# One fused Mamba and mixture-of-experts block: C rows spread by DMA, the front by chunks, one product per pair in the second batch

## The chip, the cores and the metric

One core of one Trainium2 chip. A time is the device time of one execution in microseconds (us); lower is better. TensorE, VectorE, ScalarE, GpSimd (POOL) and the DMA-issuing SyncE (SP) have an instruction queue each, run in their own order, and meet only at semaphores.

## What is computed

The input is (2, 128, 16, 16): two batches of 256 tokens with 128 channels. Cut to what matters:

```python
x = x + L0_conv(ln_c(x))                       # Mamba layer: the part that the change edits
t = t + L0_ffn(ln_t(t))                        # 8 experts, top 2, width 512, gelu
x = x + L1_conv(ln_c(x), A)                    # decay along tokens
t = t + L1_ffn(ln_t(t))                        # 16 experts, top 2, width 256

# L0_conv, per batch, T=256 tokens, D_INNER=256 (two chunks of 128), 16 states:
xin, z = split(layernorm(x) @ in_proj_w.T)
xc = silu(causal_conv4(xin) + conv_b)
dt_raw, Bm, Cm = split(xc @ x_proj_w.T, [8, 16, 16])
dt = softplus(dt_raw @ dt_proj_w.T + dt_proj_b);  A = -exp(A_log)
h_t = exp(dt_t * A) * h_(t-1) + (dt_t * xc_t) * B_t        # for each of 16 states
y_t = sum_n h_t[n] * C_t[n] + xc_t * D
out = layernorm(clamp((y * silu(z)) @ out_proj_w.T))
```

## The kernel before

**Stages.** The *front* (about 0 to 30 us) normalises both batches, builds fused convolution weights `w_tap` (in_proj times taps) and does batch 0's convolution, step sizes `dt` and rows B and C. The *scan stage* (about 30 to 110 us) walks the 16 states of batch 0 and then of batch 1 in 8 pairs each; pair m = k + 8b counts through both. Batch 1's own convolution, gate and `dt` run inside batch 0's pairs, and batch 0's output, norms and router inside batch 1's. The *expert stage* (about 110 us to the end) runs four passes of 16 units, where TensorE does three products per hidden chunk (`hidden`, L1068 to L1070) and the second layer (`output`, L1092).

**Order.** A list `plan` names steps with arguments; every engine walks the same list and runs the steps it has a function for, so the list fixes each queue's order. `b1_in`, `b1_c` and `b1_out` insert batch 1's steps into batch 0's pairs.

**A pair.** TensorE spreads two B rows over the partitions by transposing a broadcast column of `bc_tok` (`spread_b`, L968) into one PSUM bank `bc_ps[0]`, and two C rows into `bc_ps[1]` (`spread_c`). ScalarE makes the decays `da` (four Exp, L487, a ring of four buffers) and copies the C rows to `cb` (L495, a ring of two). VectorE multiplies `dtx` by the B rows (`inputs`, L674) and runs the scan (`states`, L684); in pair m it does `inputs(m+1)` ahead of `states(m)`. POOL multiplies scan and `cb` (`weigh`, L326); TensorE sums the result into y (`add`, L986), one pair later.

**Front.** TensorE spreads the taps and the dt bias by products with a single row of ones (L889, L925), and does `keep_warm` products (L875) that nobody reads. ScalarE's activation functions lie in tables, and a change of set is an ACT_TABLE_LOAD; the kernel brings one in early with a dummy activation (L419, L437). `softplus(b)` is Abs, Exp (L447), Ln (L449) on ScalarE, with the rounding error of 1 + e corrected on VectorE (L648 to L653 for batch 0; `rounding`, L664 and L665, for batch 1, whose rest, `step_1` and `step_x`, is POOL's).

## Time and profile before

| | us |
|---|---|
| median of three runs | 230.44 |
| lowest, highest | 229.32, 231.79 |
| profiled execution, its own time | 230.71 |
| its span, first to last instruction | 228.9 |

The page of the profile sums each engine's busy time, cuts the span into 40 slices, follows the chain of work that ended last, and lists groups of instructions. The trace behind it answers for a stretch: which instruction ran when on which engine, and what ended the idle time before it. Busy time is an average over stages with different limits, so each stage is read by itself. The two "x" numbers of an instruction merged with its neighbours are one start and one total.

### The profile page before, as it was taken

The page shows a single profiled execution, that of the slowest core. Times are in us where ns is not written, and L with a number is a line of the kernel's source. Part 1 is how long each engine was busy: PE and PEld are TensorE (multiplying, and loading weights), DVE is VectorE, ACT ScalarE, POOL GpSimd, SP SyncE. Part 2 cuts the span into 40 slices and gives each one's busy share as a digit, 9 for nine tenths or more (in the row PEclk, how much of TensorE's full clock was granted, in tenths as well). Part 3 has the DMA queues.
Part 4 walks back from the last instruction along what each step waited for, and adds up shares of the span by engine and source line. Part 5 has one row for each costly group of instructions (what it writes and reads, how often), then busy time and mean ns, then how long its engine had stood idle before and what let it go on. Part 6 is the DMA issues. An engine that isn't in the chain of part 4 may idle for free. (4 is left out here: it accounts for less than half of the span.)

```text
span 228.9 us, 3874 instructions
## 1 busy us (share of the span) xinstructions
PE 197.1 (86%) x1272; PEld 164.4 (72%) x1272; DVE 133.9 (59%) x312; ACT 130.1 (57%) x290; POOL 104.5 (46%) x136
## 2 busy tenths in 40 slices
PE   7987598889467785967999999969999999999993
PEld 4565477546143542435699998969998899999993
DVE  2624275998256999999327474546325774433342
ACT  2502995993994481566247774746755556455630
POOL 5301004475373978463926643542436444354410
PEclk9999959999959998899999999979999999999999
DMA  5999960000000000000000000000000000000000
GB/s 144 303 334 319 315 189 0 1 1 0 0 3 0 0 1 0 0 0 0 3 0 0 6 0 0 3 0 3 0 0 1 3 3 3 0 26 0 0 3 23
DMA packets 6164, 9.65 MB, mean 42 GB/s; under 512 B 369, under 2 KB 2937, under 8 KB 6146
## 3 DMA queue, kind: packets, MB, share of 16 engines
q1 hardware_dynamic: 6146, 9.42, 13.7%
q8 instruction: 10, 0.16, 0.3%
q14 instruction: 8, 0.07, 0.1%
HBM read 9.16 MB, written 0.26 MB: 41 GB/s over the span
## 5 line engine op out<-in xcount | busy, mean ns | idle before, releaser
L326 POOL TENSOR_TENSOR hc<-hs,cb 128x1024 f32<-128x1024 f32 x16 | 37.6, 2352 | 40.4 <-DVE hs L684 40.4
L809 DVE SCALAR_TENSOR_TENSOR acc<-dbx_ps,comb,acc 128x128 f32<-128x128 f32 x96 | 29.1, 345 | 38.0 <-PE dbx_ps L1092 36.9
L1068 PE MATMUL bc_ps<-x_hi,w_hi 128*128 128x256 f32 x128 | 42.1, 329 | 0.0
L540 ACT ACTIVATE hid<-bc_ps,par 128x256 f32<-128x256 f32 x64 | 26.9, 471 | 22.0 <-PE bc_ps L1070 21.9
L684 DVE TENSOR_TENSOR_SCAN hs<-da,dbx_ps 128x1024 f32<-128x1024 f32 x16 | 36.5, 2279 | 1.4 <-ACT da L487 0.8
L1070 PE MATMUL bc_ps<-x_hi,w_lo 128*128 128x256 f32 x128 | 36.5, 285 | 0.0
L968 PEld LDWEIGHTS bc_ps<-ident,bc_tok 128*128 128x128 f32 x128 | 16.4, 152 | 27.9 <-ACT cb L495 9.4
L1069 PE MATMUL bc_ps<-x_lo,w_hi 128*128 128x256 f32 x128 | 36.4, 284 | 0.0
L340 POOL TENSOR_TENSOR w_lo<-w1b,w_hi 128x256 fp32r<-128x256 f32 x32 | 23.5, 735 | 27.6 <-ACT w_hi L532 27.3
L968 PE MATMUL bc_ps<-ident,bc_tok 128*128 128x128 f32 x128 | 21.3, 301 | 16.8 <-DVE dbx_ps L674 7.4
L1092 PE MATMUL dbx_ps<-w2a,hid 128*128 128x128 f32 x256 | 35.0, 281 | 0.5 <-issue 0.3
L1092 PE MATMUL dbx_ps<-w2b,hid 128*128 128x128 f32 (+1 forms) x256 | 33.9, 276 | 0.5 <-DVE acc L809 0.5
L340 POOL TENSOR_TENSOR w_lo<-w1a,w_hi 128x256 fp32r<-128x256 f32 x32 | 23.2, 731 | 23.0 <-ACT w_hi L532 23.0
L1092 PEld LDWEIGHTS dbx_ps<-w2a,hid 128*128 128x128 f32 x256 | 32.2, 196 | 1.2 <-ACT hid L540 0.6
L543 ACT ACTIVATE hid<-bc_ps 128x512 f32<-128x512 f32 x32 | 19.1, 597 | 24.0 <-PE bc_ps L1070 23.9
L1092 PEld LDWEIGHTS dbx_ps<-w2b,hid 128*128 128x128 f32 x256 | 31.3, 191 | 1.0 <-issue 0.7
L487 ACT ACTIVATE da<-dt,a_neg 128x255 f32<-128x255 f32 x64 | 27.1, 497 | 0.0
L1068 PEld LDWEIGHTS bc_ps<-x_hi,w_hi 128*128 128x128 f32 x128 | 24.7, 193 | 0.6 <-issue 0.5
L1069 PEld LDWEIGHTS bc_ps<-x_lo,w_hi 128*128 128x128 f32 x128 | 24.7, 193 | 0.5 <-issue 0.5
L1070 PEld LDWEIGHTS bc_ps<-x_hi,w_lo 128*128 128x128 f32 x128 | 24.6, 192 | 0.0
L674 DVE TENSOR_TENSOR dbx_ps<-dtx,bc_ps 128x1024 f32<-128x1024 f32 x16 | 19.6, 1224 | 7.1 <-POOL dtx L362 3.7
L986 PE MATMUL y_ps<-hc,ident 128*128 128x512 f32 x32 | 17.0, 658 | 2.9 <-POOL hc L326 2.9
(164 smaller groups left out, 247.2 us busy)
## 6 DMA issues: line engine op xcount, KB each, us to landing
w1a<-w_in SPq DMA_DIRECT2D x2, 1024.0 KB, 9.5
w1b<-w_in SPq DMA_DIRECT2D x2, 1024.0 KB, 11.8
par<-packed_in SPq DMA_DIRECT2D x1, 472.0 KB, 3.5
x_cm<-x_in SPq DMA_DIRECT2D x2, 128.0 KB, 2.3
y_out<-out_sb SPq DMA_DIRECT2D x2, 128.0 KB, 1.7
w2a<-w_in SPq DMA_DIRECT2D x2, 0.5 KB, 9.8
w2b<-w_in SPq DMA_DIRECT2D x2, 0.5 KB, 10.1
row_sb<-row_in SPq DMA_DIRECT2D x1, 5.0 KB
```

Source lines behind the costliest of these rows:

```text
L326: nc.gpsimd.tensor_tensor(hc[p][:], hs[p][:], cb[p][:].rearrange("p i (o t) -> p i o t", o=1).to_broadcast([128, PAIR, DC, T]), ALU.mult). ...
L340: nc.gpsimd.tensor_tensor(w1_lo[p][:], w1[layer][:, bass.ds(u * UW, UW)], w1_hi[p][:].bitcast(F32), ALU.subtract).then_inc(s["w1_staged"], 1)
L487: ins = nc.scalar.activation(da[q][:, i, c, 1:T], dt[:, c, b, 1:T], ACT.Exp, scale=a_neg[:, c * NS + k * PAIR + i:c * NS + k * PAIR + i + 1])
L540: ins = nc.scalar.activation(hid[p][:, c, :], h_ps[:, p, T * c:T * (c + 1)], ACT.Gelu, bias=par[:, bass.ds(u * UC + at, 1)])
L674: nc.vector.tensor_tensor(dbx[p], dtx[b][:].rearrange("p (o c) t -> p o c t", o=1).to_broadcast([128, PAIR, DC, T]), rows.to_broadcast([12 ...
L684: nc.vector.tensor_tensor_scan(*flat, 0.0, ALU.mult, ALU.add).then_inc(s["h_done"], 1)
L809: nc.vector.scalar_tensor_tensor(acc[k][:, t, :], o_ps[:, w // span % RING, 128 * t:128 * (t + 1)], comb[layer][b][:, t, bass.ds(u, 1)], a ...
L968: ins = nc.tensor.transpose(bc_ps[which][:, T * i + 128 * t:T * i + 128 * (t + 1)], bc_tok[:, b, t, n:n + 1].to_broadcast([128, 128]), ide ...
L1068: nc.tensor.matmul(h_ps[:, p, T * c:T * (c + 1)], w1_hi[w][:, at], x_hi[b][:], start=True, stop=False)
L1069: nc.tensor.matmul(h_ps[:, p, T * c:T * (c + 1)], w1_hi[w][:, at], x_lo[b][:], start=False, stop=False)
L1070: ins = nc.tensor.matmul(h_ps[:, p, T * c:T * (c + 1)], w1_lo[w][:, at], x_hi[b][:], start=False, stop=True)
L1092: ins = nc.tensor.matmul(o_ps[:, bank, 128 * t:128 * (t + 1)], hid[p][:, c, 128 * t:128 * (t + 1)], w2[layer][:, bass.ds(u * UC + c, 1), : ...
```

## The change

- **C rows.** ScalarE copies the 16 C rows of a batch to `c_row` (16 partitions); SP stores them to a small DRAM tensor and loads them back, spread over 128 partitions, in three parts (pairs 0, 1 to 3, 4 to 7) into a `cb` that holds all 8 pairs. `spread_c`, the `cb` copies and their semaphores go. SP does this after the first half of layer 0's weights, and for batch 1 after all weights.
- **Front.** The taps come by a DMA that spreads one row over 128 partitions (into `cb`'s last slots) and a ScalarE copy into PSUM; the dt bias is added by ScalarE and VectorE as a column of the packed parameters. `xs_a` lives in PSUM. Four `keep_warm` products instead of nine after `rows_out`. `conv(0)` and `conv(1)` follow one another; `softplus(0)` goes by chunks of 128 channels, each in its own bank.
- **Tables** are loaded by name, without dummy activations.
- **Batch 1.** The copies `u1` and `z0` go; silu reads PSUM. `v(1)` moves from after pair 4 to after pair 2, `bc(1)` from after pair 2 to after pair 3, `bc_copy(1)` from pair 4 to pair 5 behind `softplus(1)`, `rounding` and `step_1` from after pair 5 to after pair 4, `step_x` from after pair 6 to after pair 5. `rounding` waits for Exp and not for Ln.

The diff, cut to its core:

```diff
+C_PARTS = ((0, 1), (1, 4), (4, NP))
...
-plan = [("constants",), ("x_stats", 0), ("x_stats", 1), ("rows_out",), ("x_norm", 0), ("taps", 0), ("inner_x", 0),
-        ("taps", 1), ("in_proj", 0), ("conv", 0), ("x_norm", 1), ("inner_x", 1), ("conv", 1), ("in_proj", 1),
-        ("v", 0), ("bc", 0), ("z", 0), ("softplus", 0), ("bc_copy", 0), ("z_copy",), ("first_rows",),
-        ("conv1", 0), ("second_b",), ("conv1", 1), ("second_c",)]
-b1_in = {3: [("silu1",)], 4: [("bc_copy", 1)]}
-b1_c = {1: [("conv1_copy",)], 5: [("softplus", 1)]}
-b1_out = {1: [("z", 1)], 2: [("bc", 1)], 4: [("v", 1)], 5: [("rounding",), ("step_1",)], 6: [("step_x",)]}
+plan = [("constants",), ("x_stats", 0), ("x_stats", 1), ("rows_out",), ("taps_in", 0), ("x_norm", 0), ("taps_in", 1),
+        ("taps", 0), ("inner_x", 0), ("taps", 1), ("in_proj", 0), ("x_norm", 1), ("conv", 0), ("conv", 1), ("inner_x", 1),
+        ("in_proj", 1), ("v", 0), ("bc", 0), ("softplus", 0), ("first_rows",), ("z", 0), ("conv1", 0), ("second_b",),
+        ("conv1", 1), ("first_sum",)]
+b1_in = {3: [("silu1",)], 5: [("softplus", 1), ("bc_copy", 1)]}
+b1_out = {1: [("z", 1)], 2: [("v", 1)], 3: [("bc", 1)], 4: [("rounding",), ("step_1",)], 5: [("step_x",)]}
 for k in range(NP):
-    plan += [("pair_in", 0, k)] + b1_in.get(k, []) + [("pair_c", 0, k)] + b1_c.get(k, [])
-    plan += [("pair_out", 0, k)] + b1_out.get(k, [])
+    plan += [("pair_in", 0, k)] + b1_in.get(k, []) + [("pair_out", 0, k)] + b1_out.get(k, [])
 for k in range(NP):
-    plan += [("pair_in", 1, k)] + [(name, 0, 0) for name in before_states.get(k, [])] + [("pair_c", 1, k)]
+    plan += [("pair_in", 1, k)] + [(name, 0, 0) for name in before_states.get(k, [])]
...
+    sp.dma_start(cb[:, NP - DC:NP].rearrange("p c i t -> p (c i t)"), taps.to_broadcast([C, DC * TAPS * 128])).then_inc(s["taps_loaded"], 16)
...
+    def c_rows_round(b):
+        sp.wait_ge(s["c_row_ready"], b + 1)
+        sp.dma_start(c_rows[b], c_row[:, b, :]).then_inc(s["c_row_stored"], 16)
+        sp.wait_ge(s["c_row_stored"], 16 * (b + 1))
+        for i, (k0, k1) in enumerate(C_PARTS):
+            if b:
+                sp.wait_ge(s["hc_done"], k1 + RING)
+            sp.dma_start(cb[:, k0:k1].rearrange("p k i t -> p (k i t)"),
+                         c_rows[b, PAIR * k0:PAIR * k1].rearrange("(o n) t -> o (n t)", o=1).to_broadcast([128, (k1 - k0) * PAIR * T])
+                         ).then_inc(s[f"c{i}_loaded"], 16)
+    weights(0, 0, w1_0, w2_0)
+    c_rows_round(0)
+    weights(0, 1, w1_0, w2_0)
+    for i in range(2):
+        weights(1, i, w1_1, w2_1)
+    c_rows_round(1)
...
     def weigh(b, k, p):
         m = k + NP * b
         pool.wait_ge(s["h_done"], m + (1 + RING))
-        pool.wait_ge(s["cb_done"], m + (1 + RING))
+        for i, (k0, k1) in enumerate(C_PARTS):
+            if k0 <= k < k1:
+                pool.wait_ge(s[f"c{i}_loaded"], 16 * (b + 1))
         pool.wait_ge(s["y_done"], m + 1)
         nc.gpsimd.tensor_tensor(hc[p][:], hs[p][:],
-                                cb[p][:].rearrange("p i (o t) -> p i o t", o=1).to_broadcast([128, PAIR, DC, T]),
+                                cb[:, k].rearrange("p i (o t) -> p i o t", o=1).to_broadcast([128, PAIR, DC, T]),
...
     def constants():
+        nc.scalar.preload_act_table_set("exp_and_others")
         act.wait_ge(s["params_loaded"], 16)
         nc.scalar.activation(a_neg[:], col("a_log"), ACT.Exp).then_inc(s["a_exp"], 1)
+        nc.scalar.preload_act_table_set("silu_and_others")
         act.wait_ge(s["ident_ready"], 1)
         for c in range(DC):
             ins = nc.scalar.activation(diag_d[:, c, :], ident[:], ACT.Identity, scale=col("d_skip")[:, c:c + 1])
         ins.then_inc(s["diag_ready"], 1)
-        act.wait_ge(s["ones_ready"], 1)
-        link(nc.scalar.activation(scrap[:], ones[:, 0:1], ACT.Silu))
...
+    def taps_in(c):
+        act.wait_ge(s["taps_loaded"], 16)
+        nc.scalar.activation(taps_ps[c], taps_sb[:, c, :], ACT.Copy).then_inc(s["taps_ps"], 1)
...
     def softplus(b):
         if b == 0:
-            logarithm_table()
-        act.wait_ge(s["dt_ps"], b + 1)
-        link(nc.scalar.activation(dt_a[b][:], halves(dt_ps[b]), ACT.Abs))
-        if b:
-            nc.scalar.activation(dt[:, :, b, :], halves(dt_ps[b]), ACT.Relu)
-        nc.scalar.activation(dt_e[b][:], dt_a[b][:], ACT.Exp, scale=-1.0).then_inc(s["exp_dt"], 1)
-        act.wait_ge(s["exp_dt"], b + 1)
-        nc.scalar.activation(dt_l[b][:], dt_e[b][:], ACT.Ln, bias=ones[:, 0:1]).then_inc(s["ln_dt"], 1)
+            for c in range(DC):
+                act.wait_ge(s["dt_ps"], c + 1)
+                nc.scalar.activation(dt_a[0][:, c], dt0_ps[c][:, 0:T], ACT.Abs, bias=dt_bias(c)).then_inc(s["abs_done"], 1)
+                act.wait_ge(s["abs_done"], c + 1)
+                nc.scalar.activation(dt_e[0][:, c], dt_a[0][:, c], ACT.Exp, scale=-1.0).then_inc(s["exp_dt"], 1)
+            nc.scalar.preload_act_table_set("natural_log")
+            bc_copy(0)
+            for c in range(DC):
+                act.wait_ge(s["exp_dt"], c + 1)
+                nc.scalar.activation(dt_l[0][:, c], dt_e[0][:, c], ACT.Ln, bias=ones[:, 0:1]).then_inc(s["ln_dt"], 1)
+            nc.scalar.preload_act_table_set("exp_and_others")
+            return
+        act.wait_ge(s["dt_ps"], DC + 1)
+        for c in range(DC):
+            ins = nc.scalar.activation(dt_a[1][:, c], halves(dt1_ps)[:, c, :], ACT.Abs, bias=dt_bias(c))
+        ins.then_inc(s["abs_done"], 1)
+        for c in range(DC):
+            ins = nc.scalar.activation(dt[:, c, 1, :], halves(dt1_ps)[:, c, :], ACT.Relu, bias=dt_bias(c))
+        ins.then_inc(s["relu_done"], 1)
+        act.wait_ge(s["abs_done"], DC + 1)
+        nc.scalar.activation(dt_e[1][:], dt_a[1][:], ACT.Exp, scale=-1.0).then_inc(s["exp_dt"], 1)
+        nc.scalar.preload_act_table_set("natural_log")
+        act.wait_ge(s["exp_dt"], DC + 1)
+        nc.scalar.activation(dt_l[1][:], dt_e[1][:], ACT.Ln, bias=ones[:, 0:1]).then_inc(s["ln_dt"], 1)
+        nc.scalar.preload_act_table_set("exp_and_others")
...
     def bc_copy(b):
         act.wait_ge(s["bct_ps"], b + 1)
-        nc.scalar.activation(bc_tok[:, b], bct_ps[b], ACT.Copy).then_inc(s["bct_ready"], 1)
-    def z_copy():
+        nc.scalar.activation(c_row[:, b, :], bct_ps[b][0:NS, T:2 * T], ACT.Copy).then_inc(s["c_row_ready"], 1)
+        nc.scalar.activation(b_tok[:, b], bct_ps[b][:, 0:TT * NS].rearrange("p (t r) -> p t r", t=TT),
+                             ACT.Copy).then_inc(s["bct_ready"], 1)
+    def silu1():
+        nc.scalar.preload_act_table_set("silu_and_others")
         act.wait_ge(s["z_ps"], 1)
-        nc.scalar.activation(z0[:], halves(z_ps[0]), ACT.Copy).then_inc(s["z_copied"], 1)
-    def conv1_copy():
+        nc.scalar.activation(sz[:, :, 0, :], halves(z_ps), ACT.Silu).then_inc(s["sz_ready"], 1)
         act.wait_ge(s["conv1_ps"], 1)
         for c in range(DC):
-            ins = nc.scalar.activation(u1[:, c, :], halves(conv1_ps)[:, c, :], ACT.Identity, bias=col("conv_b")[:, c:c + 1])
-        ins.then_inc(s["u1_ready"], 1)
-    def silu1():
-        act.wait_ge(s["u1_ready"], 1)
-        nc.scalar.activation(xc[:, :, 1, :], u1[:], ACT.Silu).then_inc(s["xc_ready"], 1)
-        act.wait_ge(s["z_copied"], 1)
-        nc.scalar.activation(sz[:, :, 0, :], z0[:], ACT.Silu).then_inc(s["sz_ready"], 1)
+            ins = nc.scalar.activation(xc[:, c, 1, :], halves(conv1_ps)[:, c, :], ACT.Silu, bias=col("conv_b")[:, c:c + 1])
+        ins.then_inc(s["xc_ready"], 1)
         act.wait_ge(s["z_ps"], 2)
-        nc.scalar.activation(sz[:, :, 1, :], halves(z_ps[1]), ACT.Silu).then_inc(s["sz_ready"], 1)
...
-    def c_rows(b, k, p):
-        m = k + NP * b
-        act.wait_ge(s["c_ready"], m + 1)
-        act.wait_ge(s["hc_done"], m + 1)
-        nc.scalar.activation(cb[p][:], bc_ps[1].rearrange("p (i t) -> p i t", i=PAIR),
-                             ACT.Copy).then_inc(s["cb_done"], 1)
...
     def inner_x(b):
         at = slice(TT * b, TT * (b + 1))
-        normalise(TT, xs_b[:, at, :], xs_a[:, at, :], mv[b], rstd_b[b], "rstd2", b).then_inc(s["xs_tok"], 1)
+        dve.wait_ge(s["xtok_ready"], b + 1)
+        normalise(TT, xs_b[:, at, :], xs_a[b], mv[b], rstd_b[b], "rstd2", b).then_inc(s["xs_tok"], 1)
...
-        dve.wait_ge(s["exp_dt"], 1)
-        nc.vector.scalar_tensor_tensor(dt_q[0][:], halves(dt_ps[0]), 0.0, dt_e[0][:], ALU.max, ALU.add)
-        link(nc.vector.tensor_scalar(dt_a[0][:], dt_e[0][:], 1.0, 1.0, ALU.add, ALU.subtract))
-        link(nc.vector.tensor_tensor(dt_q[0][:], dt_q[0][:], dt_a[0][:], ALU.subtract))
-        dve.wait_ge(s["ln_dt"], 1)
         for c in range(DC):
-            nc.vector.tensor_tensor(dt[:, c, 0, :], dt_q[0][:, c], dt_l[0][:, c], ALU.add).then_inc(s["dt0_ready"], 1)
+            g, low, e = dt_q[0][:, c], dt_a[0][:, c], dt_e[0][:, c]
+            dve.wait_ge(s["abs_done"], c + 1)
+            nc.vector.tensor_scalar(g, dt0_ps[c][:, 0:T], col("dt_b")[:, c:c + 1], 0.0, ALU.add, ALU.max).then_inc(s["r_done"], 1)
+            dve.wait_ge(s["exp_dt"], c + 1)
+            dve.wait_ge(s["r_done"], c + 1)
+            nc.vector.tensor_tensor(g, g, e, ALU.add)
+            link(nc.vector.tensor_scalar(low, e, 1.0, 1.0, ALU.add, ALU.subtract))
+            link(nc.vector.tensor_tensor(g, g, low, ALU.subtract))
+            dve.wait_ge(s["ln_dt"], c + 1)
+            nc.vector.tensor_tensor(dt[:, c, 0, :], g, dt_l[0][:, c], ALU.add).then_inc(s["dt0_ready"], 1)
...
     def rounding():
-        dve.wait_ge(s["ln_dt"], 2)
-        link(nc.vector.tensor_scalar(halves(y_ps), dt_e[1][:], 1.0, 1.0, ALU.add, ALU.subtract))
-        nc.vector.tensor_tensor(dt_q[1][:], halves(y_ps), dt_e[1][:], ALU.subtract).then_inc(s["rounded"], 1)
+        dve.wait_ge(s["exp_dt"], DC + 1)
+        dve.wait_ge(s["relu_done"], 1)
+        link(nc.vector.tensor_scalar(halves(f_ps), dt_e[1][:], 1.0, 1.0, ALU.add, ALU.subtract))
+        nc.vector.tensor_tensor(dt_q[1][:], halves(f_ps), dt_e[1][:], ALU.subtract).then_inc(s["rounded"], 1)
...
-        pe.wait_ge(s["ones_ready"], 1)
-        pe.wait_ge(s["row_loaded"], 16)
-        for c in range(DC):
-            nc.tensor.matmul(taps_ps[c], ones[0:1, 0:128], row_sb[0:1, DI + 512 * c:DI + 512 * (c + 1)],
-                             start=True, stop=True).then_inc(s["taps_ps"], 1)
         pe.wait_ge(s["rows_loaded"], 16)
         for c in range(DC):
             ins = nc.tensor.matmul(wv_ps[:, T * c:T * (c + 1)], rows_sb[:, 128 * c:128 * (c + 1)], rows_sb[:, DI:2 * DI],
                                    start=True, stop=True)
         ins.then_inc(s["wv_ps"], 1)
-        for sem, value in (("var1", 2), ("rstd1", 2), ("var2", 1)):
-            keep_warm(sem, value)
+        for sem, value in (("rstd1", 2), ("var2", 1)):
+            keep_warm(sem, value, 2)
...
+    def v(b):
+        if b == 0:
+            pe.wait_ge(s["wv_ready"], 1)
+            for c in range(DC):
+                pe.wait_ge(s["xc_ready"], c + 1)
+                for j in range(DC):
+                    ins = nc.tensor.matmul(dt0_ps[j][:, 0:T], w_dt[:, c, 128 * j:128 * (j + 1)], xc[:, c, 0, :],
+                                           start=(c == 0), stop=(c == DC - 1))
+                    if c == DC - 1:
+                        ins.then_inc(s["dt_ps"], 1)
+            return
+        pe.wait_ge(s["xc_ready"], DC + 1)
         for j in range(DC):
...
     def bc(b):
...
         pe.wait_ge(s["xc_ready"], DC + b)
         if b:
             pe.wait_ge(s["sz_ready"], NB)
+        else:
+            pe.wait_ge(s["xs_ready"], 1)
         w = col("xproj").rearrange("p (c r) -> p c r", c=DC)
         for t in range(TT):
             for c in range(DC):
-                ins = nc.tensor.matmul(bct_ps[b][:, t, :], xc[:, c, b, 128 * t:128 * (t + 1)], w[:, c, DTR:DTR + BC],
-                                       start=(c == 0), stop=(c == DC - 1))
+                nc.tensor.matmul(bct_ps[b][:, NS * t:NS * (t + 1)], xc[:, c, b, 128 * t:128 * (t + 1)], w[:, c, DTR:DTR + NS],
+                                 start=(c == 0), stop=(c == DC - 1))
+        for c in range(DC):
+            ins = nc.tensor.matmul(bct_ps[b][0:NS, T:2 * T], w[:, c, DTR + NS:DTR + BC], xc[:, c, b, :],
+                                   start=(c == 0), stop=(c == DC - 1))
         ins.then_inc(s["bct_ps"], 1)
...
     def z(b):
         pe.wait_ge(s["xs_ready"], 2)
         if b:
-            pe.wait_ge(s["u1_ready"], 1)
+            pe.wait_ge(s["sz_ready"], 1)
+        else:
+            pe.wait_ge(s["r_done"], DC)
         for c in range(DC):
```

## Rows read from the trace of the kernel before

**Rows 1.** Page, busy us by engine, share of the span, instructions

```profile
PE 197.1 (86%) x1272; PEld 164.4 (72%) x1272; DVE 133.9 (59%) x312; ACT 130.1 (57%) x290; POOL 104.5 (46%) x136
```

**Rows 2.** Stages: length, each engine's busy us, granted clock, DMA share, GB/s

```profile
26.00:29.00 3.00, 0.00 (x0) 0.00 (x0) 1.72 (x3) 2.96 (x5) 0.00 (x0) 0.88 1.10 340
29.00:31.00 2.00, 1.82 (x9) 1.82 (x10) 1.81 (x4) 1.97 (x5) 0.00 (x0) 0.50 1.06 300
...
64.00:67.00 3.00, 2.17 (x9) 2.10 (x10) 2.29 (x1) 3.00 (x8) 1.60 (x3) 0.50 0.02 5
...
71.00:104.00 33.00, 24.16 (x103) 13.86 (x103) 32.11 (x48) 16.75 (x41) 22.91 (x20) 0.95 0.00 0
...
116.00:146.00 30.00, 29.78 (x256) 29.21 (x256) 15.94 (x61) 20.32 (x54) 15.57 (x26) 1.00 0.01 2
```

**Rows 3.** Timeline of the front: start, total us, engine, line

```profile
5.81 0.23 ACT L413 ACTIVATE a_neg<-par 128x32 f32<-128x32 f32 x1 [3.67 <-DMA par<-packed_in]
5.94 0.68 ACT L416 ACTIVATE diag_d<-ident,par 128x128 f32<-128x128 f32 x2
...
7.50 0.65 DVE L620 TENSOR_TENSOR w_tap<-par,bc_ps 128x512 f32<-128x512 f32 x1
...
8.72 0.60 DVE L600 TENSOR_SCALAR xs_b<-xs_a,mv,rstd_b 128x128 f32<-128x128 f32 x2 [0.56 <-POOL rstd_b L298]
...
9.78 4.21 PE L875 MATMUL dbx_ps<-ident 128*128 128x128 f32 x18
...
15.29 0.44 PE L862 MATMUL dbx_ps<-ident,xs_b 128*128 128x128 f32 x2
...
16.70 2.00 PE L907 MATMUL bc_ps<-xs,w_tap 128*128 128x256 f32 x8 [0.96 <-DVE xs L605]
...
20.50 1.89 PE L907 MATMUL bc_ps<-xs,w_tap 128*128 128x256 f32 x8
...
24.45 0.60 ACT L444 ACTIVATE dt_a<-m_ps 128x512 f32<-128x512 f32 x1
...
25.06 1.28 ACT L447 ACT_TABLE_LOAD   x1
26.36 0.63 ACT L447 ACTIVATE dt_e<-dt_a 128x512 f32<-128x512 f32 x1
```

**Rows 4.** Timeline, first pairs, all engines

```profile
30.93 1.70 ACT L487 ACTIVATE da<-dt,a_neg 128x255 f32<-128x255 f32 x4
30.94 3.62 PE L907 MATMUL y_ps<-xs,w_tap 128*128 128x256 f32 x8
...
32.72 2.29 DVE L684 TENSOR_TENSOR_SCAN hs<-da,dbx_ps 128x1024 f32<-128x1024 f32 x1 [0.84 <-ACT da L487]
...
40.03 2.28 DVE L684 TENSOR_TENSOR_SCAN hs<-da,dbx_ps 128x1024 f32<-128x1024 f32 x1
...
40.17 0.65 PE L968 MATMUL bc_ps<-ident,bc_tok 128*128 128x128 f32 x4 [0.95 <-DVE dbx_ps L674]
...
40.66 1.88 PE L986 MATMUL m_ps<-hc,ident 128*128 128x512 f32 x4
...
42.34 1.23 DVE L674 TENSOR_TENSOR dbx_ps<-dtx,bc_ps 128x1024 f32<-128x1024 f32 x1
```

**Rows 5.** Timeline of VectorE, from scan 5 to scan 8

```profile
54.26 2.28 DVE L684 TENSOR_TENSOR_SCAN hs<-da,dbx_ps 128x1024 f32<-128x1024 f32 x1
61.31 0.70 DVE L664 TENSOR_SCALAR y_ps<-dt_e 128x512 f32<-128x512 f32 x1 [4.77 <-ACT dt_l L449]
...
70.35 1.23 DVE L674 TENSOR_TENSOR dbx_ps<-dtx,bc_ps 128x1024 f32<-128x1024 f32 x1 [3.69 <-POOL dtx L362]
...
75.00 2.28 DVE L684 TENSOR_TENSOR_SCAN hs<-da,dbx_ps 128x1024 f32<-128x1024 f32 x1
```

**Rows 6.** Timeline of VectorE, scan 15

```profile
107.61 2.26 DVE L684 TENSOR_TENSOR_SCAN hs<-da,dbx_ps 128x1024 f32<-128x1024 f32 x1
```

**Rows 7.** DMA issues: KB each, median us to landing

```profile
y_out<-out_sb SPq DMA_DIRECT2D x2, 128.0 KB, 1.7
```

155 lines of the change are left out of this document (63 added, 92 removed).

## Prediction

> **What bounds the kernel now.** I read the page's busy table first, then the stages, then each stage's instructions in order of time. TensorE is busy 86% of the span [rows 1], but that average mixes three stages. In the expert stage it is the bound: busy 29.78 us of 30 from 116 to 146 us [rows 2]. Nothing in that stage is edited, so whatever the stages ahead of it save should arrive at the end nearly whole. In the front, TensorE's queue decides. Nine warm-up products occupy it from 9.78 to 13.99 us, although `xs_b`, which `inner_x(0)` transposes, was finished at 9.32 [rows 3]; the transposes start at 15.29. In the scan stage VectorE is the bound where it flows: `inputs` takes 1.23 us and the scan 2.28 [rows 4], and scans 1 to 5 start at 40.03 and 54.26, four steps of 3.56 us [rows 4, 5]. It does not always flow. Scan 1 starts 7.31 us after scan 0 [rows 4], and scan 8 (batch 1's first) starts 20.74 us after scan 5 [rows 5], where three steps at 3.56 would be 10.7. In batch 1 it is full again: VectorE is busy 32.11 of the 33 us from 71 to 104 [rows 2].
>
> So the change is worth what it does in three places: ahead of scan 0, between scans 0 and 1, and between scans 5 and 8.
>
> **Front up to the first convolution.** The 1-row products of the taps, five of the nine warm-ups and the bias products leave TensorE's queue. ScalarE now feeds the taps. Its chain: the parameters arrive at 5.81, or about 5.5 since one small issue ahead of them is gone; then `a_neg` 0.23, a table load 1.28, `diag_d` 0.68, and `w_dt` and one tap copy, 0.60 each like `dt_a`, which has the same 512 columns [rows 3]. That is 8.9 us. Then VectorE: taps 0.65 and the second normalisation 0.60 [rows 3], to 10.2. From the start of the transposes to the first convolution took 16.70 − 15.29 = 1.41 us [rows 3], and I add 0.2 for colder TensorE, giving 11.8 against 16.70. The taps' own transfer (512 KB behind `par`) must land by 8.3; at the 340 GB/s of window 26:29 [rows 2] it takes 1.5 us behind `par`, so 7.0 to 7.6. At 75 GB/s (128 KB in the 1.7 us of a store, [rows 7]) it would take 7 us and cost about 4. I take the fast value, since all large loads of the trace are near it.
>
> **Convolutions to scan 0.** They now run back to back. At the higher clock one takes 1.89 us (eight pieces, [rows 3]), at the lower 3.62 [rows 4]. The warm-ups of the kernel before ran 18 pieces in 4.21 us, 0.23 each for 128 columns, while a convolution's 256-column piece took 0.24 [rows 3]: TensorE was still at half rate until about 14 us, after all that work. With five warm-ups fewer, the first convolution (11.8 to 15.3) and half the second run slow: end 18.1, activation 18.6. Both fast would be 2.5 us earlier, both slow 1.0 later. From there ScalarE's chain sets the time: table 1.28; Abs and Exp by halves, some 1.8 (they took 0.60 and 0.63 whole, [rows 3], with fixed cost twice); table 1.28; two copies 0.6; Ln halves 0.8; table 1.28; four `da` activations 1.70 [rows 4]. Sum 8.7, so scan 0 starts at 27.3 instead of 32.72 [rows 4]: **5.4 us** earlier. VectorE's halves hide under Ln and the table load. The dummy Ln and its table load are what went.
>
> The price of a table switch can be weighed. The trace shows `dt_a` done at 25.05, a load from 25.06 to 26.34 and `dt_e` from 26.36 [rows 3]: 1.28 us and no more for a switch. The Trainium skill ("ScalarE: Activation LUTs", What ACT_TABLE_LOAD costs) has 2.66 us per switch with a drain. By that, the one load less would be worth 1.4 us more; the sum goes by the row.
>
> **Scan 0 to scan 1.** The price is in TensorE's order: B rows 0, now `z(0)` (about 1.0), half of `conv1`, B rows 1, the other half, `first_sum`, B rows 2. Before, the first half ran at half rate, 3.62 us [rows 4], since TensorE had idled through 26 to 29 and the clock stood at 0.50 from 29 to 35 (the row 29:31, [rows 2]). Now TensorE ends `bc(0)` about 21.5 and is released by the B copy at 23.5, a wait of 2.0 us instead of more than 3. I take the clock as kept: halves of 1.9, B rows 2 waiting only for `inputs(1)`, scan 1 at 27.3 + 5.4 = 32.7. The gap shrinks from 7.31 to 5.4, **1.9 us**. If it falls, the gap is about 7.2 and nothing is gained. The C rows leave TensorE (four pieces, 0.65, [rows 4], per pair) and ScalarE (a copy of 512 columns, 0.60 like `dt_a`, per pair): 16 of each, but off the limiting path, as VectorE's 3.5 us per pair hides TensorE's 0.65 + 1.88 [rows 4] and ScalarE's 1.70. On their own they are worth nothing; if the clock were low the cover would be gone.
>
> **Scans 1 to 5.** The same rate, but `rounding` (two instructions, the first 0.70, [rows 5]) moves ahead of scan 5: **−1.2 us**, after 0.2 for steps at 3.5 instead of 3.56. TensorE carries 1.0, 1.9 and 1.9 us extra in pairs 1 to 3 for `z(1)`, `v(1)` and `bc(1)`; B rows 5 come just in time.
>
> **Scans 5 to 8.** Before, `v(1)` stood after pair 4, so VectorE idled 4.8 us for `ln_dt` (`rounding` starts at 61.31), and later 3.7 for `dtx` (`inputs(8)` starts at 70.35) [rows 5]. Now `v(1)` runs about 39 us, `softplus(1)` ends at about 46.5 while VectorE is in scan 4, `rounding` waits for Exp alone, and POOL's `step_1` and `step_x` fit between `weigh` 4, 5 and 6. Three steps of 3.5 plus 0.3 for `dtx`: 10.8 instead of 20.74, **10.0 us**. The moved `bc_copy(1)` stands before `da` of pair 6, which is due 4 us later. From each added wait: ScalarE's `bc_copy(1)` holds `decays` 6 only; `inner_x` on VectorE waits for `x_tok` behind the tap copy, counted above.
>
> **C rows by DMA.** SP waits for the row copy (about 23.3), stores 16 KB (1.7 as a 128 KB store, [rows 7]) and then spreads 256 KB, 768 KB and 1 MB. At 300 GB/s, with 1.7 of latency, the parts land at about 27.5, 30 and 33.5; `weigh` 0, 1 and 4 want them at 29.6, 35 and 45. Of the weights, 6 MB now stand behind them and land near 53; the first use of them is `stage` in batch 1. Batch 1's rows follow at 55 to 65, wanted at 61 and 75. All of it is hidden: cost nothing. If the cover went, `weigh` and two pairs later the scan would wait.
>
> **Batch 1.** VectorE-bound before and after: scan 15 started 107.61 − 75.00 = 32.6 us after scan 8 [rows 5, 6]. No gain.
>
> **Sum.** 5.4 + 1.9 − 1.2 + 10.0 = 16.1 us. The profiled execution took 230.71 (span 228.9 and 1.8 around it), 0.3 above the median 230.44. 230.44 − 16.1 = 214.3, and I put **214.5**.
>
> **The rivals.**
> *TensorE's clock falls* (22%). Less work on TensorE means longer gaps. For: clock 0.50 in 29:31 and 64:67 after idling [rows 2]. Against: in steady pairs it works 2.5 of 3.5 us. If it is low at the convolutions and at `conv1`, 1.0 + 1.8 are lost; if also while `v(1)` and `bc(1)` are in the queue, 2.5 to 3 more, because B rows 5 are late. Time 217 to 220. The row comes first: after the idle window the same eight pieces took 3.62 instead of 1.89. The Trainium skill ("TensorE: Matmul & The Clock Gate", Part 4) adds that transposes do not count as work for the clock; by that the removed C transposes would cost nothing here.
> *Preloads double the loads* (6%). If each named preload is followed by the load that was there anyway, three of 1.28 in front and two around `softplus(1)` are added; the latter partly hide. Gain 11, time 219.
> *No gain in the middle* (6%): another wait (`b_ready`, `hc_done`) takes the place of `ln_dt`; then only 5.4 + 1.9 − 1.2 remain, time 222 to 226.
> *The spread is slow, and the kernel slower than before* (5%). 128 destination rows read one source row of 2 to 8 KB; no transfer of the trace does that. At the 75 GB/s of [rows 7] the first 1 MB takes 14 us and lands at about 40, so `weigh(1)` is 5 late; 2 MB take 28 us, the weights 19 more, the second 2 MB 28 more: the last part lands at about 105. Then `weigh(12)` runs, about as long as a scan, scan 14 waits for it, and scan 15 starts after 110 instead of at 107.61 [rows 6]: 233 us, and each tenth of rate less adds some 6. Above 120 GB/s all is hidden, below about 80 it is slower than before. The loads at 300 to 340 GB/s speak against it [rows 2].
> *My forecast* (61%): 212 to 217.
>
> **Range and chances.** 211.5 to 221: it holds the forecast, the clock's case, the doubled loads and the fast bound of the convolutions. A difference under 1% can't be told from none. Faster by over 1%: 0.93; within 1%: 0.03; slower: 0.04; the last two are the slow spread and the low edge of the case with no gain in the middle.
>
> **What would show it.** First convolution near 11.8 and scan 0 near 27.3; TensorE's clock 1.00 while `conv1` runs; no VectorE idle of over 1 us between scans 1 and 8; scan 8 about 16 us earlier; no wait of POOL on a DMA; from scan 8 to the end the same 153.9 us. The prediction is wrong if POOL waits for `cb`, if ScalarE shows more than 10 loads (before: 12), or if batch 1's steps lengthen.

## The result, and the profile after

| | before | after |
|---|---|---|
| median, us | 230.41 (229.32 to 231.79, 4 runs) | 213.1 (212.92 to 214.37, 4 runs) |
| profiled execution, its own time | 230.71 | 212.92 |
| its span | 228.9 | 211.0 |
| scan 0 starts | 32.72 | 27.35 |
| scan 1 | 40.03 | 32.71 |
| scan 5 | 54.26 | 47.70 |
| scan 8 | 75.00 | 58.58 |
| scan 15 | 107.61 | 91.18 |
| from scan 15 to the end | 121.29 | 119.82 |

After to before is 0.926, with a 95% interval of 0.920 to 0.932. Of the 17.9 us between the two spans, 16.4 are there when scan 8 starts. Batch 1's scans take as long as before. The last 1.5 us stand behind scan 15, in the expert stage, of which the change touches only two waits.

The page of the changed kernel, busy time by engine and the slices of VectorE, granted clock and DMA. Against [rows 1] TensorE does 16.5 us less and its share of the shorter span is the same 86%:

```profile
PE 180.6 (86%) x1194; PEld 149.6 (71%) x1194; DVE 135.5 (64%) x317; ACT 120.1 (57%) x276; POOL 104.4 (49%) x136
...
DVE  2764689999899999972373846563158573433433
...
PEclk9999999999999979999999999999999999999998
DMA  6950199995540000000000000000000000000000
```

VectorE's digits are 8 and 9 from the sixth slice to the seventeenth (26 to 90 us). Its waits in the changed kernel from 27 to 92 us (engine, tile, line, what it waited for: us in total, times, longest), which is all of them:

```profile
DVE dbx_ps L702 <- PE bc_ps L996: 0.8, 1, 0.8
DVE dbx_ps L702 <- POOL dtx L379: 0.5, 1, 0.5
DVE m_ps L623 <- POOL rstd L313: 0.2, 1, 0.2
```

The same view of the kernel before, from 32 to 108 us, its largest:

```profile
DVE y_ps L664 <- ACT dt_l L449: 4.8, 1, 4.8
DVE dbx_ps L674 <- POOL dtx L362: 3.7, 1, 3.7
DVE dbx_ps L674 <- PE bc_ps L968: 3.1, 3, 2.2
```

The changed kernel by stretch, columns as in [rows 2]: scan 0 to 1, 1 to 5, 5 to 8, 8 to 15:

```profile
27.35:32.71 5.36, 3.89 (x20) 2.98 (x20) 4.55 (x4) 5.33 (x12) 2.35 (x1) 1.00 0.99 395
32.71:47.70 14.99, 13.81 (x56) 8.00 (x56) 14.85 (x11) 12.45 (x25) 9.35 (x4) 1.00 1.07 325
47.70:58.58 10.88, 7.61 (x24) 3.24 (x24) 10.25 (x7) 9.89 (x26) 9.59 (x7) 1.00 0.54 170
58.58:91.18 32.60, 22.49 (x84) 12.02 (x84) 31.82 (x48) 10.15 (x24) 21.93 (x21) 0.95 0.10 33
```

and the two stretches of the kernel before that answer to the first and the third:

```profile
32.72:40.03 7.31, 6.50 (x33) 5.37 (x31) 4.65 (x3) 4.50 (x12) 2.35 (x1) 0.84 0.01 3
...
54.26:75.00 20.74, 13.56 (x51) 8.12 (x48) 11.65 (x10) 13.65 (x27) 10.87 (x7) 0.84 0.00 1
```

Between scans 5 and 8 VectorE (the third busy number) was busy for 11.65 of 20.74 us; now for 10.25 of 10.88. The granted clock is 1.00 where it was 0.84. DMA works at 325 to 395 GB/s under scans 0 to 5, where it was idle, and nobody waits for it.

The end of the front in the changed kernel, timeline of VectorE. Nothing stands idle from 22.85 to scan 0, so VectorE's own queue sets it:

```profile
22.85 0.43 DVE L680 TENSOR_TENSOR dt<-dt_q,dt_l 128x256 f32<-128x256 f32 x1 [1.74 <-ACT dt_l L472]
23.19 0.48 DVE L673 TENSOR_SCALAR dt_q<-y_ps,par 128x256 f32<-128x256 f32 x1
23.77 0.42 DVE L676 TENSOR_TENSOR dt_q<-dt_q,dt_e 128x256 f32<-128x256 f32 x1
...
24.44 0.42 DVE L678 TENSOR_TENSOR dt_q<-dt_q,dt_a 128x256 f32<-128x256 f32 x1
24.90 0.42 DVE L680 TENSOR_TENSOR dt<-dt_q,dt_l 128x256 f32<-128x256 f32 x1
25.36 0.69 DVE L682 TENSOR_TENSOR dtx<-xc,dt 128x512 f32<-128x512 f32 x1
26.08 1.23 DVE L702 TENSOR_TENSOR dbx_ps<-dtx,bc_ps 128x1024 f32<-128x1024 f32 x1
27.35 2.29 DVE L712 TENSOR_TENSOR_SCAN hs<-da,dbx_ps 128x1024 f32<-128x1024 f32 x1
```

and of ScalarE:

```profile
17.07 0.47 ACT L452 ACTIVATE xc<-bc_ps,par 128x256 f32<-128x256 f32 x1 [1.25 <-PE bc_ps L927]
17.56 1.28 ACT L455 ACT_TABLE_LOAD   x1
...
20.61 1.28 ACT L468 ACT_TABLE_LOAD   x1
...
23.16 1.28 ACT L473 ACT_TABLE_LOAD   x1
24.46 6.58 ACT L520 ACTIVATE da<-dt,a_neg 128x255 f32<-128x255 f32 x16
```

Scan 0 needs the first four of the 16 pieces of `da`. The third and the fourth by themselves:

```profile
25.36 0.91 ACT L520 ACTIVATE da<-dt,a_neg 128x255 f32<-128x255 f32 x2
```

They end at 26.27. ScalarE was 1.1 us ahead.

### The profile page after: what moved, and what is told of

It is laid out like the page before. It is cut to its first block and busy times, and to the rows that moved or that the text cites. A ratio compares the mean times of both kernels' runs of the same rounds, so it can differ in the third digit from the quotient of the medians.

```text
span 211.0 us, 3706 instructions
## 1 busy us (share of the span) xinstructions
PE 180.6 (86%) x1194; PEld 149.6 (71%) x1194; DVE 135.5 (64%) x317; ACT 120.1 (57%) x276; POOL 104.4 (49%) x136
## 5 line engine op out<-in xcount | busy, mean ns | idle before, releaser
L343 POOL TENSOR_TENSOR hc<-hs,cb 128x1024 f32<-128x1024 f32 x16 | 37.7, 2356 | 32.6 <-DVE hs L712 32.6
L357 POOL TENSOR_TENSOR w_lo<-w1b,w_hi 128x256 fp32r<-128x256 f32 x32 | 23.5, 735 | 27.6 <-ACT w_hi L555 27.3
L1106 PE MATMUL dbx_ps<-w2a,hid 128*128 128x128 f32 x256 | 34.1, 276 | 0.5 <-issue 0.3
L566 ACT ACTIVATE hid<-bc_ps 128x512 f32<-128x512 f32 x32 | 19.1, 597 | 24.1 <-PE bc_ps L1083 23.9
L1106 PEld LDWEIGHTS dbx_ps<-w2a,hid 128*128 128x128 f32 x256 | 31.4, 192 | 1.2 <-ACT hid L563 0.6
L1106 PEld LDWEIGHTS dbx_ps<-w2b,hid 128*128 128x128 f32 x256 | 31.3, 191 | 1.1 <-issue 0.7
L520 ACT ACTIVATE da<-dt,a_neg 128x255 f32<-128x255 f32 x64 | 26.5, 493 | 2.8 <-DVE hs L712 2.7
L1081 PEld LDWEIGHTS bc_ps<-x_hi,w_hi 128*128 128x128 f32 x128 | 24.4, 191 | 0.6 <-issue 0.5
L996 PEld LDWEIGHTS bc_ps<-ident,b_tok 128*128 128x128 f32 x64 | 7.0, 141 | 21.7 <-DVE dbx_ps L702 16.9
L996 PE MATMUL bc_ps<-ident,b_tok 128*128 128x128 f32 x64 | 10.7, 292 | 13.1 <-DVE dbx_ps L702 11.5
```

Of the source, the lines that this page charges most:

```text
L343: nc.gpsimd.tensor_tensor(hc[p][:], hs[p][:], cb[:, k].rearrange("p i (o t) -> p i o t", o=1).to_broadcast([128, PAIR, DC, T]), ALU.mult). ...
L357: nc.gpsimd.tensor_tensor(w1_lo[p][:], w1[layer][:, bass.ds(u * UW, UW)], w1_hi[p][:].bitcast(F32), ALU.subtract).then_inc(s["w1_staged"], 1)
L520: ins = nc.scalar.activation(da[q][:, i, c, 1:T], dt[:, c, b, 1:T], ACT.Exp, scale=a_neg[:, c * NS + k * PAIR + i:c * NS + k * PAIR + i + 1])
L566: ins = nc.scalar.activation(hid[p][:], h_ps[:, p, :].rearrange("p (c t) -> p c t", c=UC), ACT.Gelu)
L1081: nc.tensor.matmul(h_ps[:, p, T * c:T * (c + 1)], w1_hi[w][:, at], x_hi[b][:], start=True, stop=False)
L1106: ins = nc.tensor.matmul(o_ps[:, bank, 128 * t:128 * (t + 1)], hid[p][:, c, 128 * t:128 * (t + 1)], w2[layer][:, bass.ds(u * UC + c, 1), : ...
```

## The experiments

Twelve kernels in three groups; each group ran on one chip beside the kernel before (medians 229.8, 229.57 and 229.85 us). "Yardstick" is the changed kernel as it is, run again within a group. Three things vary from run to run in unedited code and have to be kept apart from an edit. One is the first convolutions: their 16 pieces took 5.26 us in the profile above, and 5.34 to 6.39 in the profiles of the eight experiments that leave the warm-up products of the changed kernel alone. The second is the stretch from scan 15 to the end: 119.8 to 122.6 us over all twelve. The third is the front of the kernel before: scan 0 starts at 32.72 us in its own profile and at 34.42 in that of the kernel with two moved steps, whose front is the same. So the times of scans inside a profile are compared as well as medians.

**The yardsticks**

> The kernel after, unchanged, as the yardstick for the other kernels of this group: 213 us (212.9 to 214.4 so far). It also shows whether the gain ahead of scan 8 (16.4 us between the two traces) and the 1.5 us that the expert stage was shorter in the profiled execution come again; the second should not, if it is only TensorE's clock at a change of pass.

First group: 214.85 us (213.55 to 216.26), ratio 0.939 (0.934 to 0.944). Scans 0, 1, 8 and 15 at 27.75, 33.11, 58.98 and 91.57.

> The kernel after, unchanged, as the yardstick for the kernels of this group: 213 to 215 us, scan 0 at 27.3 to 27.8, scan 8 31.2 us later.

Third group: 215.88 us (214.71 to 217.45), ratio 0.938 (0.931 to 0.944). Scans at 28.74, 34.10, 59.99 and 93.19. From scan 0 to scan 14 the two are as the changed kernel above; ahead of scan 0 the convolutions differ (5.34 and 6.15 us), and in the second the step from scan 14 to 15 takes 3.1 us instead of 2.5. The gain in the median is thus 14 to 17 us.

**Does the order of batch 1's steps carry the middle?** The changed kernel with the steps of batch 1 at the places that they had before:

```diff
-        b1_in = {3: [("silu1",)], 5: [("softplus", 1), ("bc_copy", 1)]}
-        b1_out = {1: [("z", 1)], 2: [("v", 1)], 3: [("bc", 1)], 4: [("rounding",), ("step_1",)], 5: [("step_x",)]}
+        b1_in = {3: [("silu1",)], 4: [("bc_copy", 1)], 5: [("softplus", 1)]}
+        b1_out = {1: [("z", 1)], 2: [("bc", 1)], 4: [("v", 1)], 5: [("rounding",), ("step_1",)], 6: [("step_x",)]}
```

> The kernel after, with only the order of batch 1's steps put back: bc(1) after pair 2, bc_copy(1) at pair 4, v(1) after pair 4, rounding and step_1 after pair 5, step_x after pair 6. My theory (10 of the 16 us come from this order): softplus(1) starts near 48 instead of 41, the decays of pair 6 end near 55, dtx near 61, and scan 8 starts near 65.7 instead of 58.6: 7 us slower than the kernel after, 220. Rival (the stalls went because ScalarE and TensorE carry less work): order matters little, under 2 us, 213 to 215.

224.1 us (222.51 to 225.48), ratio 0.979 (0.973 to 0.985), 9.2 us over the yardstick. VectorE from scan 5 to 8, idle time in brackets:

```profile
47.52 2.28 DVE L712 TENSOR_TENSOR_SCAN hs<-da,dbx_ps 128x1024 f32<-128x1024 f32 x1
51.25 0.69 DVE L692 TENSOR_SCALAR bc_ps<-dt_e 128x512 f32<-128x512 f32 x1 [1.46 <-ACT dt_e L483]
...
56.36 2.29 DVE L712 TENSOR_TENSOR_SCAN hs<-da,dbx_ps 128x1024 f32<-128x1024 f32 x1 [2.55 <-issue]
62.33 1.23 DVE L702 TENSOR_TENSOR dbx_ps<-dtx,bc_ps 128x1024 f32<-128x1024 f32 x1 [3.68 <-POOL dtx L379]
```

Scan 8 starts at 66.97 instead of 58.98: 8.0 us, of which the three idle times are 7.7. The 3.68 behind `dtx` is the 3.7 of the kernel before [rows 5]. The second wait was 0.5 us in the kernel before: `da` of pair 6 stands on ScalarE behind `softplus(1)` and begins at 54.57. Scan 0 came 0.6 us later than in the yardstick, so 7.4 of the 8.0 lie behind scan 1. From scan 1 to scan 8 the kernel before takes 34.97 us, this one 33.26 and the yardstick 25.87: of the 9.1 us that the change gains there, 7.4 hang on the order.

**How much of it did the kernel before need nothing else for?** The kernel before with two steps moved:

```diff
-        b1_out = {1: [("z", 1)], 2: [("bc", 1)], 4: [("v", 1)], 5: [("rounding",), ("step_1",)], 6: [("step_x",)]}
+        b1_out = {1: [("z", 1)], 2: [("bc", 1)], 3: [("v", 1)], 5: [("rounding",), ("step_1",), ("step_x",)]}
```

> The kernel before, with only two steps moved: v(1) after pair 3 instead of pair 4, and step_x directly behind step_1. The bank of dt still has to be freed by bc_copy(1), so v(1) can't go earlier here. My theory: v(1) ends near 55.4 instead of 57.4, rounding starts 2 us earlier (59.3), and dtx no longer waits for weigh(6): 3.6 us. Together 5 to 5.6 us faster than before, ratio 0.977, 225. Rival (the whole 10 us needed the freed PSUM bank): no gain.

224.62 us (223.12 to 226.06), ratio 0.976 (0.969 to 0.984). From scan 0 to 8 it takes 35.95 us instead of 42.28 (changed kernel: 31.23). Its waits of VectorE from 34 to 104 us:

```profile
DVE dbx_ps L674 <- PE bc_ps L968: 4.3, 3, 2.3
DVE dbx_ps L674 <- POOL dtx L362: 1.1, 1, 1.1
```

The 4.8 for `dt_l` has gone and the 3.7 for `dtx` is 1.1, but the wait for B rows has grown from 3.1 to 4.3, 2.3 of it once, for rows that TensorE makes behind `v(1)`. Two moved steps were worth 5.0 us in the median (229.57 − 224.62). Of the 6.3 us in the profile 1.2 lie between scans 0 and 1 (6.11 us instead of 7.31), ahead of both moved steps; from scan 1 to 8 it takes 29.84 us instead of 34.97, which is 5.1. The changed kernel takes 25.87; of those 4.0 the waits for B rows are 3.5 (4.3 against 0.8). Whether the C work on TensorE or the place of the other steps in its queue made these rows late is not told apart by this kernel; the next two bear on it.

**What was the C work on TensorE and ScalarE worth?** The changed kernel with as much work added behind each pair's sum: three products of 128 columns with zeros, added into `y`, and a copy of 512 columns on ScalarE into a tile that is not read there. Both are extra; the result does not depend on them.

```diff
+                if k + NP * b + RING < NB * NP:
+                    pe.wait_ge(s["zeros_ready"], 1)
+                    for _ in range(3):
+                        nc.tensor.matmul(y_bank[b][:, 0:128], ident[:], zeros[:], start=False, stop=False)
...
+            def copy_load(b, k):
+                act.wait_ge(s["hc_done"], k + NP * b + 1)
+                link(nc.scalar.activation(hid[0][:], w_dt[:], ACT.Copy))
```

> The kernel after, with the work of the C rows put back as a load that nobody reads: behind every pair's sum TensorE adds three products with zeros of 128 columns (0.65 us), and behind every pair's decays ScalarE waits for the hc_done that the C copy waited for and copies 512 columns (0.6 us). The rows themselves still come by DMA. My theory (the C rows were off the limiting path): no change beyond 1%, 213 to 214.5. Rival (freeing both engines is what brought the gain): 16 times up to 0.6 us, 218 or more.

217.2 us (215.06 to 218.0), ratio 0.946 (0.940 to 0.951); yardstick 214.85. Then only the products on TensorE:

> The kernel after, with only TensorE's part of the C load put back (three products with zeros of 128 columns behind every pair's sum), and nothing on ScalarE. Theory (the load itself costs half a microsecond where B rows 5 come late behind v(1); the rest of the 2 us that the load on both engines showed is TensorE's clock during conv1): 0.5 us above the yardstick, and the stretch from scan 1 to scan 8 takes 26.4 instead of 25.87. Rival (each of the 16 loads delays a pair): 2 us or more.

216.58 us (215.52 to 217.46), ratio 0.941 (0.935 to 0.946); yardstick 215.88. In both profiles scan 1 to 8 takes 26.4 us, against 25.9 in both yardsticks. And from scan 8 to 15 both take 32.6, as the yardstick of the first group. The 0.5 is one wait (VectorE, in the kernel with both loads; the same instruction of the other waits 0.51 too):

```profile
44.45 1.23 DVE L708 TENSOR_TENSOR dbx_ps<-dtx,bc_ps 128x1024 f32<-128x1024 f32 x1 [0.51 <-PE bc_ps L1002]
```

Between scans 1 and 15 TensorE's part costs 0.5 us and ScalarE's copy nothing. The span of the kernel with both loads is 3.1 us over its yardstick's: 0.4 ahead of scan 0, 1.2 between scans 0 and 1, these 0.5, and 0.9 behind scan 15. The loads leave one thing out. The real C rows were handed from TensorE to ScalarE and their bank handed back, pair by pair, and what that coupling cost was not tested. Both profiles show another 1.2 to 1.5 us between scans 0 and 1 (6.6 and 6.8 instead of 5.36). TensorE in the kernel with the products alone:

```profile
27.35 3.62 PE L929 MATMUL bc_ps<-xs,w_tap 128*128 128x256 f32 x8
...
34.48 0.83 PE L1042 MATMUL m_ps<-zeros,ident 128*128 128x128 f32 x6
```

The first half of `conv1` ran at half rate, as in [rows 4] (granted clock 0.70 from 22 to 28 us and 0.67 from 28 to 33; the yardstick has 0.72 and 1.00, and its half took 2.11). The first added product starts at 34.48, behind it, so the load did not cause that. It is the rival "TensorE's clock falls", seen at last, at 1.2 and 1.5 us of the 1.8 predicted for `conv1`. A lower clock ahead of `conv1` is no rarity. Three of the nine other profiles of the changed kernel and its variants have it, for 3.4 us (in the second yardstick 0.50 from 24.1 to 27.5 us), and there it is over before the first half of `conv1` ends, with 5.36 or 5.37 us between scans 0 and 1 all the same. In the two load kernels it lasts 6.9 us (in the one with the products alone from 24.4 to 31.3). Why it lasts longer in just these two is open; both also have one more memset early in GpSimd's queue.

**Do the three parts of the spread matter?** The changed kernel with one part of 2 MB:

```diff
-C_PARTS = ((0, 1), (1, 4), (4, NP))
+C_PARTS = ((0, NP),)
```

> The kernel after, with the C rows of a batch spread by one DMA of 2 MB instead of three parts of 256 KB, 768 KB and 1 MB. The store ends near 23.7 us and 2 MB should land near 32.5, so weigh(0) starts 3 us later than now (29.71), but only scan 2 (36.2) waits for it: no change, 213. For batch 1 the DMA waits for all of batch 0's weigh and lands near 67, while weigh(8) wants the rows at 61: scan 10 (67.1) waits until about 69.5, 2 to 3 us slower if nothing takes it up, 215 to 216. Rival (the landing of the rows sets the pace already in the kernel after): 3 us per batch, 219.

220.0 us (217.21 to 222.91), ratio 0.957 (0.951 to 0.963), 5.1 over the yardstick. GpSimd:

```profile
32.15 2.35 POOL L343 TENSOR_TENSOR hc<-hs,cb 128x1024 f32<-128x1024 f32 x1 [17.24 <-DMA cb<-c_rows]
...
57.76 2.36 POOL L343 TENSOR_TENSOR hc<-hs,cb 128x1024 f32<-128x1024 f32 x1 [1.21 <-DVE hs L712]
...
67.06 4.64 POOL L343 TENSOR_TENSOR hc<-hs,cb 128x1024 f32<-128x1024 f32 x2 [5.58 <-DMA cb<-c_rows]
```

In batch 0 `weigh(0)` comes at 32.15 instead of about 30, and no scan is later (scan 8 at 58.90). In batch 1 the one transfer has to wait until `weigh(7)` has left the whole of `cb` at 60.1 and lands at 67.1; the hold reaches scan 10 (+2.0) and scan 11 (+3.9), and stays 3.9 to the end of the stage. This profile is of the fastest of six executions (217.21 us); why others took up to 222.91 is not shown, so 3.9 of the 5.1 are explained. In the changed kernel SP issues batch 1's parts from 52.34 on, one behind the other, as the pairs leave their part of the tile. So the split buys nothing at the start and some 4 us at the change of batch.

**The warm-up products.** Nine instead of four behind the tap rows in the changed kernel, and four instead of nine in the kernel before:

```diff
-                for sem, value in (("rstd1", 2), ("var2", 1)):
-                    keep_warm(sem, value, 2)
+                for sem, value in (("var1", 2), ("rstd1", 2), ("var2", 1)):
+                    keep_warm(sem, value)
```

> The kernel after, with the nine warm-up products of the kernel before. They occupy TensorE to about 10.6 instead of 9.0, 0.5 us behind the arrival of xs_b (10.05), and the higher clock comes sooner: the two convolutions take 4.2 to 4.8 instead of 5.3. Together between 0.5 faster and 0.5 slower, 212.6 to 213.6. Rival (the cut of the warm-ups was worth 2 us or more in the new front as well): 215.

212.18 us (211.53 to 214.58), ratio 0.926 (0.917 to 0.936). No yardstick ran on its chip, so the scans decide. TensorE with nine:

```profile
6.27 4.21 PE L902 MATMUL dbx_ps<-ident 128*128 128x128 f32 x18
...
11.84 3.72 PE L927 MATMUL bc_ps<-xs,w_tap 128*128 128x256 f32 x16 [0.96 <-DVE xs L628]
```

and in the changed kernel:

```profile
6.85 2.17 PE L902 MATMUL dbx_ps<-ident 128*128 128x128 f32 x8 [0.44 <-POOL rstd L313]
...
11.77 5.26 PE L927 MATMUL bc_ps<-xs,w_tap 128*128 128x256 f32 x16 [0.97 <-DVE xs L628]
```

A product is two pieces here. The first convolution starts at the same time (11.84 and 11.77), since TensorE has to wait for VectorE anyway, which multiplies the taps ahead of `xs`; with nine both convolutions run at the full rate. Scan 0 comes at 25.99 instead of 27.35, scan 8 at 57.22 instead of 58.58. Against the yardsticks' scan 0 (27.75 and 28.74) the gain is larger.

> The kernel before, with four warm-up products in the front instead of nine. My theory (TensorE's queue held the front): the transposes of inner_x(0) start 2.3 us earlier, near 13, the first convolution runs at the lower clock and gives back up to 1.7, and scan 0 starts 0.5 to 2 us earlier: 228.5 to 230. Rival (the warm-ups were needed): the clock costs more than the queue gives, 231 or more.

228.02 us (226.48 to 230.19), ratio 0.994 (0.989 to 0.998); scan 0 at 32.15 instead of 32.72. There the nine stood in TensorE's way. The first convolution starts at 15.19 instead of 16.70 but then takes 3.78, at the lower rate, and 0.6 us is left at scan 0. That profile is of the slowest of ten executions, and 0.6 is less than scan 0 moves by itself (32.72 and 34.42), so the gain rests on the median: 1.6 us.

**What sets scan 0: ScalarE's tables or VectorE's queue?** One table set that has both Exp and Ln, so that the four switches between them go:

```diff
-                    nc.scalar.preload_act_table_set("exp_and_others")
+                    nc.scalar.preload_act_table_set("natural_log_exp_and_others")
...
-                    nc.scalar.preload_act_table_set("natural_log")
...
-                    nc.scalar.preload_act_table_set("exp_and_others")
```

> The kernel after, with one table set that holds Exp and Ln in place of the two sets (natural_log, exp_and_others) around softplus: two loads of 1.28 us fewer on the chain to scan 0, and two fewer around softplus(1), which are hidden. My theory (ScalarE's chain sets scan 0): scan 0 at 25.0 to 25.3 instead of 27.35, where VectorE's chain (Abs, Exp, the three corrections by halves, Ln) may take over and keep 0.5 of it: 1.8 to 2.4 us faster, 211. Rival (something else, the B rows or VectorE, ends at the same time): under 0.5 us.

213.19 us (212.65 to 215.95, the last of which is the profiled one), ratio 0.929 (0.922 to 0.936). From the end of the convolutions to scan 0 it takes 9.2 us instead of 10.3: of two loads, 2.56 us, only 1.1 is gained. VectorE, now with a wait of 0.62 where it had 1.74 and its queue full from there on:

```profile
23.08 0.43 DVE L676 TENSOR_TENSOR dt<-dt_q,dt_l 128x256 f32<-128x256 f32 x1 [0.62 <-ACT dt_l L471]
...
27.58 2.29 DVE L708 TENSOR_TENSOR_SCAN hs<-da,dbx_ps 128x1024 f32<-128x1024 f32 x1
```

The opposite edit, VectorE's four corrections of both halves ahead of the first sum that waits for Ln:

```diff
+                for c in range(DC):
                     dve.wait_ge(s["ln_dt"], c + 1)
-                    nc.vector.tensor_tensor(dt[:, c, 0, :], g, dt_l[0][:, c], ALU.add).then_inc(s["dt0_ready"], 1)
+                    nc.vector.tensor_tensor(dt[:, c, 0, :], dt_q[0][:, c], dt_l[0][:, c], ALU.add).then_inc(s["dt0_ready"], 1)
```

> The kernel after, with VectorE's order in softplus(0) changed: all corrections of both chunks first, then the two sums with Ln. Theory (VectorE's queue, not ScalarE's, sets scan 0: chunk 1's four instructions, 1.6 us, stand behind the wait for chunk 0's Ln): inputs(0) ends near 26.0 and scan 0 waits for da instead, ready at 26.1: scan 0 starts at 26.2 instead of 27.35 (1.2 us earlier), time 1 to 1.5 below the yardstick. Rival (ScalarE's chain sets it, as the prediction had it): no change.

214.77 us (213.43 to 216.85), ratio 0.932 (0.926 to 0.939); yardstick 215.88. From the end of the convolutions to scan 0: 9.65 us, 0.65 less. Scan 0 is now released by the other engine:

```profile
28.09 2.29 DVE L713 TENSOR_TENSOR_SCAN hs<-da,dbx_ps 128x1024 f32<-128x1024 f32 x1 [1.06 <-ACT da L520]
```

VectorE idles 1.06 us. The third and fourth piece of `da` by themselves:

```profile
26.68 0.89 ACT L520 ACTIVATE da<-dt,a_neg 128x255 f32<-128x255 f32 x2
```

They end at 27.57, so the other 0.5 us stand behind `da`, and no row shows what they were for. That half microsecond is why the edit gave 0.65 and not some 1.1, by which ScalarE was ahead. From the end of the convolutions VectorE's `inputs(0)` ends 1.7 us earlier than in the changed kernel (27.03 − 18.44 = 8.6 against 27.31 − 17.03 = 10.3), while ScalarE's fourth `da` ends after 9.1 in place of 9.2. So there are two chains close together, VectorE's the longer in the changed kernel, and each edit alone gains only part of what it takes off one. Together, with the nine warm-ups:

> The kernel after, with three edits together: VectorE's corrections ahead of Ln, one table set with Exp and Ln for softplus (four loads fewer), and nine warm-up products. Theory: the convolutions save 1.6 us, then from their end to scan 0 it takes 7.5 us instead of 10.3: scan 0 at about 23.2 to 23.6 instead of 27.4, everything behind it shifted, 4 us below the yardstick, 210. If the C rows' DMA then ends last (row copy 2.5 us earlier too) weigh(0) still finds them. Rival (the gains of the three hide behind one another): under 2 us.

212.0 us (210.26 to 212.9), ratio 0.919 (0.913 to 0.925), the fastest of all, and 3.9 under the yardstick on the same chip, which ran from 214.71. Scan 0 at 24.79, 8.7 after the convolutions, which take 3.72. VectorE's `dt` still releases ScalarE's `da`:

```profile
22.00 0.76 DVE L677 TENSOR_TENSOR dt<-dt_q,dt_l 128x256 f32<-128x256 f32 x2
...
22.53 6.48 ACT L516 ACTIVATE da<-dt,a_neg 128x255 f32<-128x255 f32 x16 [1.08 <-DVE dt L677]
```

## Why the prediction was right, and where it was not

**Front up to the first convolution.** Predicted 11.8, measured 11.77. ScalarE's chain and the taps' transfer, 5.2 us for 512 KB behind the parameters, were sized right, and the transfer is hidden.

**Convolutions to scan 0.** Predicted 27.3, measured 27.35, by two errors that cancel. The convolutions ended at 17.0 and not at 18.1: half rate for less of them than I took. ScalarE's chain from the activation's end (17.5) to its fourth `da` (26.3) took 8.7 us, where the sum had 8.7. But the step "VectorE's halves hide under Ln and the table load" failed. Only the first half hides. VectorE's queue takes the second half's four corrections (from 23.19) after the first half's sum, which waits for Ln until 22.85; they cost 1.7 us on the path and scan 0 came 1.1 behind ScalarE. The match to 0.05 us is luck. I had priced one engine's chain and only named the other. The order of the waits within VectorE's queue was in the diff, and writing its ten instructions down behind the time of Ln would have shown it. The kernels with one table set and with Ln last show it from both sides.

The prediction's table loads hold: ten instead of twelve, each 1.28 us, the next activation 0.01 to 0.02 us behind. The 2.66 us per switch of the Trainium skill ("ScalarE: Activation LUTs", What ACT_TABLE_LOAD costs) are a load of 1.28, which agrees with every row, and a drain of some 1.38, which shows in none. By its 2.66 the set with both functions should have gained 5.3 us ahead of scan 0, an estimate; it gained 1.1, though VectorE's chain would have capped either price.

**Scan 0 to scan 1.** Predicted 5.4, measured 5.36, with the clock at 1.00 as taken. The two kernels with the C load had it low and 6.6 and 6.8 us, so the 22% for the clock was no empty case. The 7.31 of the kernel before varies with the clock too: 7.22 and 6.11 in the two other profiles of that code, so the gain here is 0.8 to 2.0 us. Whether transposes count as work for the clock, as the prediction quotes, no run here shows: what the load kernels add are plain products.

**Scans 1 to 5 and 5 to 8.** Predicted 1.2 more (from 14.23) for the moved `rounding`, measured 0.76; predicted 10.8, measured 10.88. The two waits named are the two that went (0.5 of the second is left), and the order of the steps carries 7.4 of the 9.1 us between scans 1 and 8.

**C rows.** "On their own they are worth nothing" was short by 0.5 us, the wait for B rows 5 behind `v(1)`, of which I wrote that they "come just in time". In the medians the loads cost 0.7 us (products alone) and 2.4 (with the copies), but with intervals that touch the yardsticks', and with the low clock in the profiles. That the spread costs nothing is right with the three parts as they are; with one part it would not be.

**Warm-ups.** I counted five of them as 4.9 us of gain together with the rest of TensorE's queue and never asked what they still did in the new order. There they ran in time that was free, and to drop them cost 1.4 us at scan 0 from profile to profile.

**Batch 1 and the end.** 32.60 us as predicted (32.6). "From scan 8 to the end the same 153.9 us" is 152.4. The 1.5 us stands behind scan 15, and that stretch ran from 119.8 to 122.6 us in the twelve experiments, none of which edits it. The granted clock goes with it. In the kernel before it falls once in the expert stage, for some 3.5 us (columns as in [rows 2]):

```profile
151.10:154.60 3.50, 3.50 (x20) 3.50 (x19) 0.90 (x4) 1.94 (x5) 0.73 (x1) 0.51 0.00 0
```

Seven of the fourteen profiles have such a stretch behind scan 15 and ahead of the last microseconds, and take 121.3 to 122.6 us from scan 15 to the end. The other seven, the changed kernel's among them, have none and take 119.8 to 120.6. Both sorts stand among the kernels with the change and among those without it. So it is no part of the change: sum 16.1 predicted, 16.4 measured up to scan 8, and the 213.1 stands 1.4 under the 214.5 by the luck of that stretch. Three of its four executions had a mean granted clock of 0.988 (212.92 to 213.11 us), the fourth 0.968 (214.37). The later medians of 214.85 and 215.88 lie on the other side.

## What to carry to other kernels

Where a step is cut into halves to overlap two engines, write down both queues in order with each wait at its place: the second half of one engine stands behind the first half's last wait. Before work is moved off an engine, ask whether the order of the steps alone brings the gain; here moving two steps gave a third of it. An edit that pays in one order of the queue (fewer warm-ups) may cost in another, so after a large change the small ones are to be priced again.

## What the runs showed of the hardware

A DMA that spreads one DRAM row of 2 to 8 KB over 128 partitions ran faster than the weight loads of the same kernel: 381 to 397 GB/s in the stretches in which it runs, ahead of the weights, with the DMA engines 99% busy, against 300 to 340 before [rows 2]; 2 MB landed in 7.4 us in the kernel with one part. DMA issues of the changed kernel, KB each and median us to landing:

```profile
cb<-c_rows SPq DMA_DIRECT2D x2, 1024.0 KB, 6.8
...
cb<-c_rows SPq DMA_DIRECT2D x2, 768.0 KB, 5.2
...
cb<-c_rows SPq DMA_DIRECT2D x2, 256.0 KB, 3.8
```

The rival of 75 GB/s, taken from a 128 KB store [rows 7], was far off: the first 16 KB store of the C rows took 1.45 us from its issue at 22.30 to the next issue, which waits for its landing, so most of the 1.7 us of the 128 KB store is not rate. The granted clock stands at 1.00 while TensorE's pieces still take twice their time, as in the kernel before ahead of 14 us [rows 3]. The two convolutions of the changed kernel, columns as in [rows 2]:

```profile
11.77:14.90 3.13, 3.13 (x7) 2.52 (x8) 1.81 (x8) 0.38 (x1) 0.94 (x2) 1.00 0.50 138
14.90:17.03 2.13, 2.13 (x12) 1.82 (x11) 0.68 (x2) 0.47 (x1) 0.00 (x0) 1.00 0.00 0
```

